# Second choices scattered during the expert stage, a fourth buffer for weight pieces, and counts made while PE sums

## The chip, the core and the metric

One core of a Trainium2 chip runs the whole program in one launch. The metric is the device time of an execution in microseconds; three runs of the kernel before took 1609.75, 1610.61 (the median) and 1611.9 us. One further execution was recorded by the hardware profiler; its rows are the ones shown here.

## The reference, cut to what matters

The input is x of shape (128, 256, 9, 9). A convolutional token mixer comes first and gives x again; it is not touched by the change. Then each of the 128*81 = 10368 tokens of 256 values goes through a mixture of experts with eight experts:

```python
t = _to_tokens(x)                                  # (128, 81, 256)
xf = _ln_t(t).reshape(n, 256)                      # n = 10368
probs = softmax(xf @ Wr.T + br)                    # 8 experts
top2_prob, top2_idx = top_k(probs, 2)
comb = zeros((n, 8)).at[arange(n)[:, None], top2_idx].add(top2_prob)
h = gelu(einsum('nd,edh->enh', xf, W1) + b1, approximate=False)   # hidden 512
o = einsum('enh,ehd->end', h, W2) + b2
t = t + einsum('ne,end->nd', comb, o)
```

Only the two chosen experts of a token count, so the kernel computes 20736 rows rather than 8*10368.

## The kernel before, in words

Each engine has its own program; they meet in semaphores. After the mixer (up to about 734 us) two stages follow that the change touches, and a last one that adds the two results of each token (from 1503 us).

**Routing stage.** A pixel q (0 to 80) is a block of 128 tokens, one for each image. The pixels go in batches of 6, six times 12, and 3 (`BATCHES`, `FIRST`), and every engine walks the batches j = 0 to 7. PE turns two pixels (a pair) at a time and multiplies them with the router (`turn_pair`); ACT writes the turned pair back (`turned`, L1385); DVE makes its statistics (`pixel_parts`, L1050), the variance (`pixel_variance`), the logits and the two choices (`choice_logits`, `choices`, which ends with L1112, the counts of the batch per expert). PE sums these counts over the 128 images (`places`), and DVE makes of them the position of each token in its expert's region (`positions`: L1120 adds the base, L1122 adds pixel after pixel, L1129 and L1130 write the integer indices). ACT then normalises the pixel's rows into one of 18 ring slots (`row`, L1414 and L1416), and POOL scatters that slot twice into `rows_d` in DRAM, once by the first choice and once by the second (L1549). A row has 256 values and a tag of four words (position, token, weights).

In the same stage the weights come in: 32 pieces of 128x512. SP loads a piece into one of three buffers (L381), ACT rounds it to a high half (`high_piece`, L1423), DVE makes the low half (`low_piece`, L1042), which frees the buffer. In batch j ACT rounds piece 4j after `deviations`, and pieces 4j+1 to 4j+3 at the batch's end; as there are three buffers, 4j+3 can only be loaded when low piece 4j, the last thing DVE does in the batch, is done.

At the end DVE makes a table with the row start and the expert of each of 88 tiles of 256 rows (L1156 to L1180), SP writes a tile of empty rows behind each region (L387, L389), and SP, DVE wait for all scatters (`scat0` to `scat17`) before a tile is read.

**Expert stage.** For each of the 88 tiles SP loads 256 rows (`load_rows`, L400) into one of two slots, as soon as PE has turned the tile two before (`tt_p`) and DVE has copied its tags (`tag_c`, L1196, after the result of two tiles before, L1231). PE turns the rows (L685), multiplies up (L701) and down (L716); it is one tile ahead with the up product. ACT makes high halves (L1458) and gelu (L1466), DVE low halves (L1190, L1223) and the result (L1231), ACT weights it (L1473), and POOL scatters it to its tokens with two indirect DMAs (`return_rows`, L1558). The result has two slots: DVE waits for the return of two tiles before (`yst`), ahead of L1204.

Of the kernel before, what the change touches and what calls it, by code (L numbers as in the profile page):

```python
# [55 lines left out]
def metaformer_kernel(nc, x, taps, tap_bn, tap_rows, toeplitz_mask, ident, band_masks, rot_masks, zstrings,  # L56
# [14 lines left out]
    with ctx:  # L71
# [14 lines left out]
        y_d = dram("y_d", [2 * TOKENS, C])  # L86
        u_d = dram("u_d", [HW, 128, 136])
# [48 lines left out]
        def take_aux(parts, *dims, dt=fp32):  # L136
# [9 lines left out]
            if len(dims) > 1:  # L146
# [61 lines left out]
        stage_s = pool_[:, stage_at:stage_at + 3 * PIECE].rearrange("p (a n) -> p a n", a=3)  # L208
# [3 lines left out]
        base_s = sb("base_s", [128, EXPERTS])  # L212
# [3 lines left out]
        til_s = sb("til_s", [128, 4, EXPERTS])  # L216
# [9 lines left out]
        hot_s = take_aux(128, 3, WIDEST, EXPERTS)  # L226
        top_s = take_aux(128, 5, WIDEST)
        tot_s = take_aux(128, EXPERTS)
        at_s = take_aux(128, WIDEST, EXPERTS)
        pick_s = take_aux(128, 2, WIDEST, EXPERTS)  # L230
        tab_s = take_aux(1, 4, TILES)
        tcmp_s = take_aux(1, 2, TILES, EXPERTS)
# [5 lines left out]
        hh_s = take_aux(128, 2, 2, KB, SLOTS, dt=fp16)  # L238

# [6 lines left out]
                   l2_p l2m_c e_c band_p x1_c phase_a wst_in0 wst_in1 wst_in2 whi_c wlo_c b2_in rm_p rw_c  # L246
                   blk_p part_c turned_c lgr_c var2_c ln_c rstd_c nmr_c probs_c ex2_c tot_c tri_p xft_c idx_c
                   """ + " ".join(f"scat{k}" for k in range(RING)) + """ yw_c ends_c base_c pad_out tab_r rin0 rin1 tt_p xhi_c xlo_c h_p
# [13 lines left out]
        def landed(q):  # L262
            return 32 * (q // RING + 1)
# [15 lines left out]
        def _(sp):  # L279
# [97 lines left out]

            for n in range(PIECES):
                if n >= 3:
                    sp.wait_ge(S["wlo_c"], n - 2)  # L380
                sp.dma_start(stage_s[:, n % 3], ffn_w[n]).then_inc(S[f"wst_in{n % 3}"], 16)  # L381
# [10 lines left out]
            for k in range(RING):  # L392
                sp.wait_ge(S[f"scat{k}"], landed(HW - RING + (k - HW) % RING))
            sp.wait_ge(S["base_c"], 1)
# [8 lines left out]

            load_rows(0, 0)
            load_rows(1, 1)
            for t in range(2):
                sp.wait_ge(S["tt_p"], t + 1)
                sp.wait_ge(S["tag_c"], t + 1 + CREDIT)
                load_rows(t + 2, t)
            with sp.Fori(1, TILES // 2 - 1) as i:  # L410
                for par in range(2):
                    t = i * 2 + par
                    sp.wait_ge(S["tt_p"], t + 1)
                    sp.sem_inc(S["settle_s"], 1)
                    sp.wait_ge(S["tag_c"], t + 1 + CREDIT)
                    load_rows(t + 2, par)
# [20 lines left out]
        def _(pe):  # L437
# [224 lines left out]
            def places(j):  # L662

                pe.wait_ge(S["tot_c"], j + 1)
                nc.tensor.matmul(ps[:, 7, 0:EXPERTS], before_s[:, :], tot_s[:, :], start=True, stop=True)  # L665
                nc.tensor.matmul(ps[:, 7, EXPERTS:2 * EXPERTS], ones_s[:, :], tot_s[:, :],
                                 start=True, stop=True).then_inc(S["tri_p"], 1)
# [85 lines left out]
        def _(dve):  # L753
# [280 lines left out]
            link(nc.vector.tensor_copy(base_s[:, :], region_s[:, :]))  # L1034

            def low_piece(n):

                if n < 0 or n >= PIECES:
                    return
                dve.wait_ge(S["whi_c"], n + 1)  # L1040
                cols = slice(n * PIECE, (n + 1) * PIECE)
                nc.vector.scalar_tensor_tensor(w_s[:, 1, cols], stage_s[:, n % 3], WSCALE, w_s[:, 0, cols],  # L1042
                                               ALU.mult, ALU.subtract).then_inc(S["wlo_c"], 1)
# [43 lines left out]
            def choices(j):  # L1087
# [23 lines left out]
                link(nc.vector.tensor_tensor(hot_s[:, 2, 0:n, :], hot_s[:, 0, 0:n, :], hot_s[:, 1, 0:n, :], ALU.add))  # L1111
                nc.vector.reduce_sum(tot_s[:, :], hot_s[:, 2, 0:n, :].rearrange("p s e -> p e s"),  # L1112
                                     axis=AX.X).then_inc(S["tot_c"], 1)

            def positions(j):

                lo, hi = FIRST[j], FIRST[j + 1]
                n = hi - lo
                dve.wait_ge(S["tri_p"], j + 1)
                link(nc.vector.tensor_tensor(at_s[:, 0, :], base_s[:, :], ps[:, 7, 0:EXPERTS], ALU.add))  # L1120
                for s in range(n - 1):
                    link(nc.vector.tensor_tensor(at_s[:, s + 1, :], at_s[:, s, :], hot_s[:, 2, s, :], ALU.add))  # L1122
                start(nc.vector.tensor_tensor(base_s[:, :], base_s[:, :], ps[:, 7, EXPERTS:2 * EXPERTS], ALU.add))
                for k in range(2):
                    ins = nc.vector.tensor_tensor(pick_s[:, k, 0:n, :], at_s[:, 0:n, :], hot_s[:, k, 0:n, :], ALU.mult)
                link(ins)
                nc.vector.reduce_sum(ptag_s[:, lo:hi, 0], pick_s[:, 0, 0:n, :], axis=AX.X)
                link(nc.vector.reduce_sum(top_s[:, 0, 0:n], pick_s[:, 1, 0:n, :], axis=AX.X))
                nc.vector.tensor_copy(idx_s[:, 0, lo:hi], ptag_s[:, lo:hi, 0])  # L1129
                nc.vector.tensor_copy(idx_s[:, 1, lo:hi], top_s[:, 0, 0:n]).then_inc(S["idx_c"], 1)  # L1130
# [6 lines left out]
            for j in range(len(BATCHES)):  # L1137
                pixel_parts(j + 1, 0)
# [13 lines left out]
            nc.vector.tensor_copy(tili_s[:, 1, :], base_s[:, :]).then_inc(S["ends_c"], 1)  # L1152
            for n in range(4 * len(BATCHES) - 3, PIECES):
                low_piece(n)
            cnt, tiles, ends = (til_s[:, k, :] for k in range(3))
            link(nc.vector.tensor_tensor(cnt, base_s[:, :], region_s[0:128, :], ALU.subtract))  # L1156
            link(nc.vector.tensor_scalar(cnt, cnt, float(SLOTS - 1), None, ALU.add))
            link(nc.vector.tensor_copy(tili_s[:, 0, :], cnt))
            link(nc.vector.tensor_scalar(tili_s[:, 0, :], tili_s[:, 0, :], SLOTS.bit_length() - 1, None,
                                         ALU.arith_shift_right))  # L1160
            link(nc.vector.tensor_copy(tiles, tili_s[:, 0, :]))
            link(nc.vector.tensor_copy(ends, tiles))
            for e in range(1, EXPERTS):
                link(nc.vector.tensor_tensor(ends[:, e:e + 1], ends[:, e:e + 1], ends[:, e - 1:e], ALU.add))


            full = [1, TILES, EXPERTS]
            link(nc.vector.tensor_tensor(tcmp_s[:, 0], ends[0:1, :].unsqueeze(1).to_broadcast(full),
                                         turn_s[:, :].unsqueeze(2).to_broadcast(full), ALU.is_le))
            link(nc.vector.tensor_tensor(tcmp_s[:, 1], tcmp_s[:, 0], tiles[0:1, :].unsqueeze(1).to_broadcast(full), ALU.mult))  # L1170
            nc.vector.reduce_sum(tab_s[:, 0, :], tcmp_s[:, 0], axis=AX.X)
            link(nc.vector.reduce_sum(tab_s[:, 1, :], tcmp_s[:, 1], axis=AX.X))
            nc.vector.tensor_scalar(tab_s[:, 2, :], tab_s[:, 0, :], float(EXPERTS), float(SLOTS), ALU.is_lt, ALU.mult)
            link(nc.vector.tensor_tensor(tab_s[:, 1, :], turn_s[:, :], tab_s[:, 1, :], ALU.subtract))
# [6 lines left out]

            for k in range(RING):
                dve.wait_ge(S[f"scat{k}"], landed(HW - RING + (k - HW) % RING))
            dve.wait_ge(S["pad_out"], 16 * (EXPERTS + 1))
# [87 lines left out]
        def _(act):  # L1272
# [134 lines left out]
            def row(j, q):  # L1407
# [4 lines left out]
                if q >= RING:  # L1412
                    act.wait_ge(S[f"scat{slot}"], landed(q - RING))
                nc.scalar.activation(xf_s[:, slot, 0:C], pixel_block(q), ACT.Identity,  # L1414
# [3 lines left out]
            def high_piece(n):  # L1418

                if n >= PIECES:  # L1420
                    return
                act.wait_ge(S[f"wst_in{n % 3}"], 16 * (n // 3 + 1))
                nc.scalar.activation(w_s[:, 0, n * PIECE:(n + 1) * PIECE], stage_s[:, n % 3], ACT.Copy,  # L1423
# [6 lines left out]
            for j in range(len(BATCHES)):  # L1430
                pairs = pairs_of(j + 1, 0) + pairs_of(j + 1, 1)
                left = list(range(FIRST[j], FIRST[j + 1]))
                for pair in pairs[:BANKS - 1]:
                    turned(pair)
                for pair in pairs[BANKS - 1:]:
# [11 lines left out]
                for n in range(4 * j + 1, 4 * j + 4):  # L1447
                    high_piece(n)
            for n in range(4 * len(BATCHES), PIECES):
# [48 lines left out]
        def _(pool):  # L1498
# [47 lines left out]
            for q in range(HW):  # L1546
                pool.wait_ge(S["xft_c"], q + 1)
                for k in range(2):
                    nc.gpsimd.indirect_dma_start(  # L1549
                        out=rows_d[:, :], out_offset=bass.IndirectOffsetOnAxis(ap=idx_s[:, k, q:q + 1], axis=0),  # L1550
                        in_=xf_s[:, q % RING, :], in_offset=None).then_inc(S[f"scat{q % RING}"], 16)
# [10 lines left out]
            with pool.Fori(0, TILES // 2) as i:  # L1562
# [99 lines left out]
```

## Time and profile before

| | us |
|---|---|
| median of three runs | 1610.61 |
| profiled execution, its time | 1601.33 |
| its span, first to last instruction | 1599.6 |
| routing stage in it | 734 to 985 |
| expert stage in it | 985 to 1503 |

In the span PE is busy 81%, DVE 68%, ACT 48%, POOL 36%. These are means over stages with different limits, so the rows that matter are those of one stage, one batch or one tile. A line of a timeline gives the start, the time from there to the end, engine, line, operation, destination and sources, the number of instructions merged, and in brackets the idle time of the engine before it with what ended it. Most timeline durations overlap the next instruction by some 0.1 us.

### The profile page before, as it was taken

What the parts mean: (1) busy time and instruction counts of PE and PEld (TensorE: products, weight loads), DVE (VectorE), ACT (ScalarE), POOL (GpSimd) and SP (SyncE); (2) the same over time, 40 slices, a digit from 0 to 9 for tenths busy, and PEclk for the clock granted to TensorE, in tenths of its full rate; (3) what the DMA queues carried; (4) which work ended last, traced back from release to release, by engine and by line L of the source; (5) the groups of instructions that cost most, each with busy time, mean ns of one, the idle gap of its engine ahead of it and who ended that gap; (6) DMA issues with size and microseconds to landing.
All of it is one profiled execution on the core that took longest, in us unless ns stands there. A gap on an engine that the chain in (4) does not pass through costs nothing.

```text
span 1599.6 us, 36879 instructions
## 1 busy us (share of the span) xinstructions
PE 1297.4 (81%) x9796; PEld 1072.9 (67%) x9797; DVE 1080.9 (68%) x2553; ACT 771.0 (48%) x1828; POOL 568.3 (36%) x561
## 2 busy tenths in 40 slices
PE   0197999999999999977656403999999999999592
PEld 0196999857676666657556302888888888888441
DVE  6797555378878788884656662777777777777462
ACT  0295666455444544442677761544555555555200
POOL 0163111333444334430577773333333333333200
PEclk9998999999999999985555555999999999999897
DMA  8635783858877978741243453222222222222297
GB/s 325 143 89 225 304 320 135 246 140 187 190 183 179 209 175 192 178 105 47 82 151 130 150 192 114 89 83 87 92 93 93 85 90 93 89 87 77 99 424 310
DMA packets 256214, 251.16 MB, mean 157 GB/s; under 512 B 149753, under 2 KB 234190, under 8 KB 251876
## 3 DMA queue, kind: packets, MB, share of 16 engines
q1 hardware_dynamic: 235789, 197.20, 41.1%
q0 software_dynamic: 20320, 53.45, 9.7%
q8 instruction: 18, 0.29, 0.1%
q14 instruction: 21, 0.17, 0.0%
q10 hardware_dynamic: 66, 0.05, 0.0%
HBM read 152.34 MB, written 105.75 MB: 161 GB/s over the span
## 4 chain that ended last, share of the span: by engine, by line
PE 56%; DVE 16%; DMA 10%; issue 6%; ACT 4%; SPq 3%; POOL 2%; DVEq 1%; ACTq 0%; POOLq 0%
PE ps L716 15%; PE ps L701 14%; PE ps L520 5%; PE ps L500 4%; PE ps L539 3%; DMA u_d<-in_zstrings 3%; PE ps L685 2%; DMA pool_<-k_d 2%; DMA pool_<-y_d 2%; POOL rows_d L1549 2%; PE ps L566 2%; SPq L291 2%; DMA pool_<-in_ffn_w 2%; PE ps L489 2%; ACT aux L1414 2%
## 5 line engine op out<-in xcount | busy, mean ns | idle before, releaser
L1558 POOL DMA_INDIRECT y_d<-pool_,to_s x176 | 173.5, 986 | 357.3 <-ACT pool_ L1473 328.0
L716 PE MATMUL ps<-pool_,aux 128*128 x2112 | 246.9, 273 | 4.9 <-DVE aux L1223 3.2
L701 PE MATMUL ps<-aux,pool_ 128*128 128x256 f16 x2112 | 247.1, 274 | 0.8 <-ACT aux L1466 0.6
L716 PEld LDWEIGHTS ps<-pool_,aux 128*128 128x128 f16 x2112 | 199.0, 98 | 47.4 <-issue 23.6
L701 PEld LDWEIGHTS ps<-aux,pool_ 128*128 x2112 | 207.2, 98 | 25.6 <-issue 1.4
L1549 POOL DMA_INDIRECT rows_d<-aux,idx_s x162 | 158.6, 979 | 105.7 <-ACT aux L1416 60.8
L1466 ACT ACTIVATE aux<-ps,b_s 128x256 f32<-128x256 f32 x352 | 138.1, 474 | 92.6 <-DVE aux L1223 92.5
L1458 ACT ACTIVATE aux<-ps 128x512 f16<-128x512 f32 x88 | 52.5, 597 | 187.0 <-PE ps L685 187.0
L1543 POOL DMA_DIRECT2D pool_<-v_d x64 | 50.0, 781 | 214.6 <-PE ps L599 213.2
L1231 DVE SCALAR_TENSOR_TENSOR pool_<-ps,pool_ 128x512 f32<-128x512 f32 x88 | 60.8, 691 | 92.4 <-PE ps L716 92.4
L539 PE MATMUL ps<-pool_,se_w_s 81*81 81x512 f32 x256 | 115.5, 593 | 3.6 <-DMA pool_<-k_d 3.6
L1223 DVE TENSOR_TENSOR aux<-aux 128x1024 f16<-128x1024 f32 x88 | 107.8, 1225 | 3.1
L1371 ACT ACTIVATE pool_<-ps,pool_ 128x81 f32<-128x81 f32 x256 | 79.5, 336 | 52.1 <-DVE pool_ L932 52.1
L883 DVE COPY aux<-ps 81x512 f32<-81x512 f32 x64 | 44.0, 687 | 71.5 <-PE ps L500 71.4
L685 PE MATMUL ps<-ident_s,pool_ 128*128 128x128 f32 x352 | 53.9, 276 | 44.1 <-DMA pool_<-rows_d 44.1
L520 PE MATMUL ps<-pool_,aux 82*128 82x162 f32 x512 | 85.6, 309 | 0.0
L1050 DVE BATCH_NORM_STATS2 aux<-big 128x6 f32<-128x256 f32 x81 | 45.0, 603 | 58.7 <-ACT big L1385 58.7
L665 PE MATMUL ps<-aux,before_s 128*128 128x8 f32 x16 | 4.8, 371 | 97.2 <-DVE aux L1112 97.2
L1473 ACT ACTIVATE pool_<-pool_,wrow_s 128x256 f32<-128x256 f32 x176 | 78.9, 498 | 9.1 <-DVE pool_ L1231 9.1
L1359 ACT ACTIVATE pool_<-ps,sa_ab 128x324 f32<-128x324 f32 x64 | 39.7, 620 | 86.6 <-PE ps L551 86.6
L1525 POOL COPY aux<-big 128x324 f32 x64 | 29.2, 457 | 138.6 <-PE ps L500 129.0
L1190 DVE TENSOR_TENSOR aux<-ps,aux 128x512 f16<-128x512 f32 x88 | 60.1, 683 | 24.8 <-ACT aux L1458 24.8
(204 smaller groups left out, 2974.4 us busy)
## 6 DMA issues: line engine op xcount, KB each, us to landing
pool_<-rows_d SPq DMA_DIRECT2D x88, 260.0 KB
pool_<-y_d SPq DMA_DIRECT2D x18, 1152.0 KB, 12.9
big<-in_x SPq DMA_DIRECT2D x2, 5184.0 KB, 21.2
xn_d<-big SPq DMA_DIRECT2D x8, 1296.0 KB, 4.8
v_d<-aux SPq DMA_DIRECT2D x64, 162.0 KB, 2.5
ks_d<-aux SPq DMA_DIRECT2D x64, 162.0 KB, 3.1
pool_<-xn_d SPq DMA_DIRECT2D x32, 324.0 KB
pool_<-k_d SPq DMA_DIRECT2D x32, 324.0 KB
```

What stands on the lines that cost most here:

```text
L500: last = nc.tensor.matmul(ps[0:HW, 4 + par, c * BS:(c + 1) * BS], xq_s[:, par, c, :], ident_s[:, :], start=True, stop=True)
L520: last = nc.tensor.matmul(o, pt_s[:, par, c, :], m_s[:, side, k * QUAD + c, :, :] .rearrange("p v n -> p (v n)"), start=True, stop=True)
L539: last = nc.tensor.matmul(ps[0:HW, n, :], se_w1_s[:, k, :], kq_s[:, par, k, 2 * n:2 * n + 2, :].rearrange("p b j -> p (b j)"), start=k == ...
L685: last = nc.tensor.transpose(ps[:, par, h * SLOTS + s * 128:h * SLOTS + (s + 1) * 128], rin_s[:, par, s, h * 128:(h + 1) * 128], ident_s[: ...
L701: last = nc.tensor.matmul(o, w_s[:, a, bass.ds(e * (4 * PIECE) + (k * HID + j * 128), 128)], xh_s[:, par, b, k * SLOTS:(k + 1) * SLOTS], s ...
L716: last = nc.tensor.matmul(ps[:, 6 + par, s * C:(s + 1) * C], hh_s[:, par, a, j, s * 128:(s + 1) * 128], w_s[:, b, bass.ds(e * (4 * PIECE) ...
L1223: nc.vector.tensor_tensor(lo, hf_s, hi, ALU.subtract).then_inc(S["hlo_c"], 1)
L1371: ins = nc.scalar.activation(e_s[:, par, h, b, :], ps[:, 2 + h, b * HW:(b + 1) * HW], ACT.Exp, bias=sm_s[:, par, 2, j:j + 1], accum_out=sm ...
L1466: nc.scalar.activation(hf_s[:, j * SLOTS:(j + 1) * SLOTS], ps[:, 2 + 2 * par + j // 2, (j % 2) * SLOTS:(j % 2 + 1) * SLOTS], ACT.Gelu, bia ...
L1473: ins = nc.scalar.activation(yo_s[:, par, s, :], yo_s[:, par, s, :], ACT.Copy, scale=wrow_s[:, par, s:s + 1])
L1549: nc.gpsimd.indirect_dma_start(out=rows_d[:, :], out_offset=bass.IndirectOffsetOnAxis(ap=idx_s[:, k, q:q + 1], axis=0), in_=xf_s[:, q % RI ...
L1558: nc.gpsimd.indirect_dma_start(out=y_d[:, :], out_offset=bass.IndirectOffsetOnAxis(ap=to_s[:, par, k:k + 1], axis=0), in_=yo_s[:, par, k, ...
```

## The change

Four things change. (1) In the routing stage POOL scatters each pixel by its first choice only, and SP also copies the rows, three pixels at a time, to a DRAM tensor `xrow_d` (`keep_rows`). The second choices get their places behind the first choices of their expert. In the expert stage the tiles are ordered so that tiles with first choices only come first; there are at least 33 of them (`SURE`). During these SP loads the kept rows back, three pixels at a time into two buffers (`load_late`), and POOL scatters them between its returns. (2) There are four buffers for weight pieces; ACT rounds pieces 4j-3 to 4j-1 after the third turned pair, and only 4j after `deviations`. (3) Positions are counted for first and second choices apart, 16 columns wide, and the sums within a batch are made before the wait for PE. (4) The table has 16 groups (full tiles of first choices, then the rest), and a pass over all pixels then adds to each second position the number of first choices of its expert (`idx2f_c`), before DVE lets PE start (`tab_r`).

```diff
+STAGED = 4
+THIRD = 3
+LATE = HW // THIRD
+SURE = -(-(BS * HW - EXPERTS * (SLOTS - 1)) // SLOTS)
+        def late_before(t):
+            return min(HW, 2 * THIRD + (HW - 2 * THIRD) * t // (SURE - 4))
+        def late_turn(b):
+            return 1 + min(t for t in range(SURE) if late_before(t) >= (b - 1) * THIRD)
...
@@ SP, routing stage @@
-            for n in range(PIECES):
-                if n >= 3:
-                    sp.wait_ge(S["wlo_c"], n - 2)
+            def load_piece(n):
+                if n >= STAGED:
+                    sp.wait_ge(S["wlo_c"], n - STAGED + 1)
...
+            def keep_rows(q):
+                sp.wait_ge(S["xft_c"], q + THIRD)
+                slot = q % RING
+                sp.dma_start(xrow_d[q:q + THIRD].rearrange("q b c -> b q c"),
+                             xf_s[:, slot:slot + THIRD, :]).then_inc(S[f"rst{slot // THIRD}"], 16)
+            for j in range(len(BATCHES)):
+                for n in range(4 * j, 4 * j + 4):
+                    load_piece(n)
+                for q in range(FIRST[j], FIRST[j + 1], THIRD):
+                    keep_rows(q)
@@ SP, expert stage @@
+            def load_late(b):
+                if b >= 2:
+                    sp.wait_ge(S[f"late_out{b % 2}"], b // 2 * (16 * THIRD))
+                sp.dma_start(late_s[:, b % 2], xrow_d[b * THIRD:(b + 1) * THIRD].rearrange("q b c -> b q c")
+                             ).then_inc(S[f"late_in{b % 2}"], 16)
+            def next_rows(t, par):
+                sp.wait_ge(S["tt_p"], t + 1)
+                sp.sem_inc(S["settle_s"], 1)
+                sp.wait_ge(S["tag_c"], t + 1 + CREDIT)
+                load_rows(t + 2, par)
             load_rows(0, 0)
             load_rows(1, 1)
+            sp.wait_ge(S["idx2f_c"], 1)
+            for b in range(2):
+                load_late(b)
+            for t in range(SURE - 2):
+                next_rows(t, t % 2)
+                for b in range(2, LATE):
+                    if late_turn(b) == t:
+                        load_late(b)
+            for k in range(2):
+                sp.wait_ge(S[f"late_out{k}"], 16 * THIRD * len(range(k, LATE, 2)))
...
@@ DVE, positions @@
+                start(nc.vector.memset(at_s[:, 0], 0.0))
+                link(nc.vector.tensor_copy(at_s[:, 1], hot_s[:, :, 0, :]))
+                for s in range(1, n - 1):
+                    link(nc.vector.tensor_tensor(at_s[:, s + 1], at_s[:, s], hot_s[:, :, s, :], ALU.add))
+                pixel_parts(j + 1, 0)
                 dve.wait_ge(S["tri_p"], j + 1)
...
@@ DVE, behind the table @@
+            wide = [128, HW, EXPERTS]
+            link(nc.vector.tensor_tensor(spread_s, pos2_s[:, :].unsqueeze(2).to_broadcast(wide),
+                                         region_s[:, :].unsqueeze(1).to_broadcast(wide), ALU.is_ge))
+            link(nc.vector.tensor_tensor(spread_s, spread_s, starts[:, full_ones].unsqueeze(1).to_broadcast(wide), ALU.mult))
+            link(nc.vector.reduce_sum(moved, spread_s, axis=AX.X))
+            link(nc.vector.tensor_tensor(moved, moved, pos2_s[:, :], ALU.add))
+            nc.vector.tensor_copy(idx_s[:, 1, :], moved).then_inc(S["idx2f_c"], 1)
...
@@ ACT @@
                 for pair in pairs[:BANKS - 1]:
                     turned(pair)
+                for n in range(4 * j - 3, 4 * j):
+                    high_piece(n)
                 for pair in pairs[BANKS - 1:]:
...
-                for n in range(4 * j + 1, 4 * j + 4):
-                    high_piece(n)
@@ POOL @@
             for q in range(HW):
                 pool.wait_ge(S["xft_c"], q + 1)
-                for k in range(2):
...
+            pool.wait_ge(S["idx2f_c"], 1)
+            sent = 0
+            for t in range(SURE - SURE % 2):
+                for q in range(sent, late_before(t)):
+                    b = q // THIRD
+                    pool.wait_ge(S[f"late_in{b % 2}"], 16 * (b // 2 + 1))
+                    nc.gpsimd.indirect_dma_start(
+                        out=rows_d[:, :], out_offset=bass.IndirectOffsetOnAxis(ap=idx_s[:, 1, q:q + 1], axis=0),
+                        in_=late_s[:, b % 2, q % THIRD, :], in_offset=None).then_inc(S[f"late_out{b % 2}"], 16)
+                sent = late_before(t)
+                return_rows(t, t % 2)
```

## Rows read from the trace of the kernel before

**Rows 1.** Busy time by stretches: us, engine busy (instructions), granted clock, DMA share, GB/s.

```profile
853.00:882.00 29.00, 16.22 (x76) 15.82 (x76) 18.33 (x70) 20.82 (x40) 22.17 (x23) 0.50 0.42 142
...
1100.00:1130.00 30.00, 29.96 (x271) 26.05 (x270) 22.19 (x54) 15.69 (x38) 9.84 (x10) 1.00 0.27 88
```

**Rows 2.** The chain of waits in order of time: start, us, what.

```profile
979.16 2.43 DMA rows_d<-aux,idx_s
...
982.88 0.42 SPq L400
```

**Rows 3.** Timeline of PE, its first expert tile.

```profile
985.55 1.08 PE L685 MATMUL ps<-ident_s,pool_ 128*128 128x128 f32 x4 [43.69 <-DMA pool_<-rows_d]
```

**Rows 4.** The scatters' source line: ns min/median/max, first and last start; their landing.

```profile
L1549 POOL DMA_INDIRECT rows_d<-aux,idx_s x162: 956/960/1365, 759.8 to 979.2; - x162
...
DMA to landing us min/median/max: 2.4/2.4/4.6
```

**Rows 5.** Timeline of DVE, the counts that end a batch's choices.

```profile
751.23 0.24 DVE L1112 TENSOR_REDUCE aux<-aux 128x8 f32<-128x48 f32 x1
...
776.50 0.32 DVE L1112 TENSOR_REDUCE aux<-aux 128x8 f32<-128x96 f32 x1
...
805.35 0.32 DVE L1112 TENSOR_REDUCE aux<-aux 128x8 f32<-128x96 f32 x1
...
922.11 0.32 DVE L1112 TENSOR_REDUCE aux<-aux 128x8 f32<-128x96 f32 x1
...
940.60 0.18 DVE L1112 TENSOR_REDUCE aux<-aux 128x8 f32<-128x24 f32 x1
```

**Rows 6.** Timeline of ACT: rows, turned pairs and roundings.

```profile
758.65 0.80 ACT L1414 ACTIVATE aux<-big,aux 128x256 f32<-128x256 f32 x1
...
761.15 0.80 ACT L1414 ACTIVATE aux<-big,aux 128x256 f32<-128x256 f32 x1
...
780.16 0.63 ACT L1423 ACTIVATE pool_<-pool_ 128x512 f16<-128x512 f32 x1 [7.12 <-DMA pool_<-in_ffn_w]
...
793.17 1.06 ACT L1385 ACTIVATE big<-ps 128x512 f32<-128x512 f32 x1
...
945.36 1.67 ACT L1423 ACTIVATE pool_<-pool_ 128x512 f16<-128x512 f32 x3
```

**Rows 7.** Timeline of DVE, the tile table.

```profile
955.51 0.16 DVE L1156 TENSOR_TENSOR til_s<-base_s,region_s 128x8 f32<-128x8 f32 x1
...
956.74 1.39 DVE L1164 TENSOR_TENSOR til_s<-til_s 128x1 f32<-128x1 f32 x7
...
958.16 0.88 DVE L1168 TENSOR_TENSOR aux<-til_s,turn_s 1x704 f32<-1x704 f32 x1
```

**Rows 8.** Source line L399, the read of a tile's row start.

```profile
L399 SPq TENSOR_LOAD <-tabi_s x88: 262/270/290, 982.1 to 1483.8; - x88
```

**Rows 9.** Timeline of SP, the empty rows behind the regions.

```profile
952.91 9.28 SPq L387 DMA_DIRECT2D rows_d<-aux  x8
```

**Rows 10.** Timeline, POOL's first return, and all engines in one later tile.

```profile
1003.13 1.00 POOL L1558 DMA_INDIRECT y_d<-pool_,to_s  x1 [23.02 <-ACT pool_ L1473]
...
1102.39 2.81 PE L716 MATMUL ps<-pool_,aux 128*128 x24
...
1106.25 0.90 ACT L1473 ACTIVATE pool_<-pool_,wrow_s 128x256 f32<-128x256 f32 x2
...
1106.77 1.22 DVE L1223 TENSOR_TENSOR aux<-aux 128x1024 f16<-128x1024 f32 x1
...
1107.00 0.40 SPq L400 DMA_DIRECT2D pool_<-rows_d  x1
...
1108.03 0.98 POOL L1558 DMA_INDIRECT y_d<-pool_,to_s  x1 [3.62 <-ACT pool_ L1473]
...
1108.15 2.81 PE L716 MATMUL ps<-pool_,aux 128*128 x24
```

**Rows 11.** Source line L1204: ns min/median/max, first and last start.

```profile
L1204 DVE TENSOR_SCALAR here_s<-tag_s,region_s x88: 217/492/506, 996.7 to 1503.0; 128x2 f32<-128x2 f32 x88
```

More of the change, by code:

```diff
@@ L393, in _ @@
                 sp.wait_ge(S[f"scat{k}"], landed(HW - RING + (k - HW) % RING))
+            for g in range(RING // THIRD):
+                sp.wait_ge(S[f"rst{g}"], kept(g))
             sp.wait_ge(S["base_c"], 1)
@@ L1151, in _ @@
             nc.vector.tensor_copy(zero_s[:, :, C + 1:C + 2], pad_s[:, :].unsqueeze(2))
-            nc.vector.tensor_copy(tili_s[:, 1, :], base_s[:, :]).then_inc(S["ends_c"], 1)
+            firsts, starts, ends, weighted = (til_s[:, k, :] for k in range(4))
+            full_ones, rest = slice(0, EXPERTS), slice(EXPERTS, 2 * EXPERTS)
+            last_row = ends[:, full_ones]
+            link(nc.vector.tensor_tensor(firsts[:, full_ones], base_s[:, 0], region_s[0:128, :], ALU.subtract))
+            link(nc.vector.tensor_tensor(last_row, base_s[:, 1], firsts[:, full_ones], ALU.add))
@@ L1153, in _ @@
+            nc.vector.tensor_copy(tili_s[:, 1, :], last_row).then_inc(S["ends_c"], 1)
             for n in range(4 * len(BATCHES) - 3, PIECES):
                 low_piece(n)
[L1155 to L1160, printed above, removed]
@@ L1170, in _ @@
[L1170 to L1174, printed above, removed]
+            counts = weighted[:, full_ones]
@@ new lines, in _ @@
+            link(nc.vector.tensor_tensor(counts, last_row, region_s[0:128, :], ALU.subtract))
+            link(nc.vector.tensor_scalar(counts, counts, float(SLOTS - 1), None, ALU.add))
+            for value, tiles in ((firsts[:, full_ones], starts[:, full_ones]), (counts, starts[:, rest])):
+                link(nc.vector.tensor_copy(tili_s[:, 0, :], value))
+                link(nc.vector.tensor_scalar(tili_s[:, 0, :], tili_s[:, 0, :], SLOTS.bit_length() - 1, None,
+                                             ALU.arith_shift_right))
+                link(nc.vector.tensor_copy(tiles, tili_s[:, 0, :]))
@@ new lines, in _ @@
+            link(nc.vector.tensor_tensor(starts[:, rest], starts[:, rest], starts[:, full_ones], ALU.subtract))
+            link(nc.vector.tensor_copy(ends, starts))
+            for e in range(1, 2 * EXPERTS):
+                link(nc.vector.tensor_tensor(ends[:, e:e + 1], ends[:, e:e + 1], ends[:, e - 1:e], ALU.add))
+            link(nc.vector.tensor_scalar(weighted, starts, -1.0, None, ALU.mult))
+            behind = slice(EXPERTS - 1, 2 * EXPERTS - 1)
+            link(nc.vector.tensor_tensor(weighted[:, behind], weighted[:, behind], starts[:, full_ones], ALU.add))
@@ new lines, in _ @@
+            behind, one_less = slice(EXPERTS, 2 * EXPERTS - 1), slice(0, EXPERTS - 1)
+            link(nc.vector.tensor_tensor(weighted[:, behind], weighted[:, behind], starts[:, one_less], ALU.subtract))
+            full = [1, TILES, 2 * EXPERTS]
+            link(nc.vector.tensor_tensor(tcmp_s, ends[0:1, :].unsqueeze(1).to_broadcast(full),
+                                         turn_s[:, :].unsqueeze(2).to_broadcast(full), ALU.is_le))
+            link(nc.vector.reduce_sum(tab_s[:, 0, :], tcmp_s, axis=AX.X))
@@ L1446, in _ @@
                     row(j, q)
[L1447 to L1449 removed]
+            for n in range(4 * len(BATCHES) - 3, PIECES):
                 high_piece(n)
```

105 lines of the change are left out of this document (56 added, 49 removed).

## Prediction, made before the changed kernel ran

> **What bounds the kernel now.** I read the busy time by stretches first, then the chain of waits, then single batches and tiles. Two stages concern the change. In the routing stage (about 733 to 985 us) POOL is the full engine: in 29 us it runs 23 scatters, one per 1.26 us, which is one of 0.96 us and a gap of 0.3, while PE, at granted clock 0.50, ACT and DVE have idle time [rows 1]. It has 162 to run, the last begins at 979.16, lands 2.43 later, and the first expert tile is on PE at 985.55 [rows 2 to 4]. The rows themselves are made faster: choices end (the end of L1112, called T below) at 751.47, 776.82, 805.67, ..., 922.43 and 940.78, so 145.6 us for five batches of twelve [rows 5]. The expert stage is PE's: 271 matmuls in 30 us, 52 a tile, is 5.76 us a tile with PE busy throughout [rows 1]. The profiled execution took 1601.33 us, its span of 1599.6 and 1.7 around it that the change does not touch; the median of the runs is 1610.61, 9.3 above; I sum differences in the profiled one and take them off the median.
>
> **Routing, the loop.** Before, after T a batch goes: a low piece that frees a buffer, the load of the next weight piece, and ACT, idle for it, rounds it from 780.16 to 780.79, T+3.97; only then pairs are turned, places counted, rows made. The last pair is turned at 794.23, T+17.4, and from there to the next T it is 11.44 [rows 5, 6]. After, a fourth buffer means pieces 4j-3 to 4j were loaded in the batch before, so ACT does not wait. It turns pair one before T, and pairs two and three as PE delivers them; the batch that has no such wait shows the third done at T+7.18 (758.65 less 751.47) [rows 5, 6]. Then come the three roundings, 1.67, then three times two rows and a pair, 2.50 each (758.65 to 761.15) [rows 6]. 7.18+1.67+7.50 = 16.35, so 1.1 earlier. The counts now run while PE sums, but that is off the path: a low piece, the sums of one batch, the statistics of a pair, offsets and picks, by the small operations' 0.2 each and some 1.1 for the statistics an estimated 5.9, put the indices at T+5.9, and ACT asks for them at T+8.9. One add of 0.29 less and a reduce twice as wide (estimated +0.16) give -0.13. Five batches: 16.35+11.44-0.13 = 27.66 each, 138.3, against 145.6: **-7.3**. Bounds: 0 if the roundings cost all that the wait did; -15 if they fall into ACT's gaps and PE's delivery sets the pace. The value lies between because they sit behind the third pair, where ACT has no gap left. To the last batch (922.43 to 940.78) nothing is rounded ahead of the first pair any more, and few rows follow: the T+3.97 counts nearly whole, **-3.9**.
>
> **Routing, the end.** Before, from 940.78 to 985.55 it is 44.8 us, and POOL's remaining scatters set it. After, POOL's 81 scatters need 102 us (81 times 1.26) in a stage of over 200, and its last follows the last row by a few us. What is late next is ACT, then DVE. From T of the last batch: ACT still has ten rows of the batch before (0.80 each [rows 6], done at T+4.7), three roundings, two rows, a rounding, a row, three roundings: T+11.1. DVE fills its zeros and makes the last low pieces until T+12.6. Then the tile table: six small operations took 1.23 (955.51 to 956.74), seven chained sums 1.39, and passes over 1x704 0.88 each [rows 7]. After, 13 small ones make 2.6, 15 sums 3.1, four passes over 1x1408, about 1.72 each, 6.9, and ten small ones behind them 2.0: 14.6. So the table is ready at T+27.2. The new places of the second choices (three passes over 648, estimated 0.8 each from the 704 ones, and four small operations: 3.4) and some 26 passed waits (about 1) come before DVE releases PE: T+31.6. SP's path is shorter: the load takes 0.8 to issue (982.1 to 982.88) and 2.67 to reach PE [rows 2, 3, 8], T+30.7. The pads also move out of POOL's cover: nine issues, eight of them 9.28 us [rows 9], from T+10.8 and a landing near 2.9 end at T+24.5, 2.7 before they would count. 44.8-31.6 = **-13.2**. Bounds -9 (pads and rows slower) to -17. Routing in all -7.3-3.9-13.2 = **-24.4**.
>
> **Expert stage.** The 81 second scatters come back here: six before the first tile, 75 over the next 29, 2.6 a tile, and SP issues 27 loads of three rows between its own. The six hide before the first results: POOL's first return came 17.6 us after PE's first tile (1003.13) [rows 10]. Per tile POOL then has two returns and 2.6 scatters, 4.6 times 1.27 = 5.84, against PE's 5.76: just full, with a lag of a few us that the two-tile slot of the results can absorb. The price is in SP's queue. A late load waits until the three scatters that read its buffer have landed, and the next tile's rows stand behind it on SP. Take 0 at the end of PE's second product of a tile, 1105.20 [rows 10]. ACT weights until 1107.15, +1.95; POOL wakes 0.28 later (written out, with constant waits; in the loop it is 0.88, 1107.15 to 1108.03), and two returns take 2.55: the first late scatter starts at +4.8. Landing 2.4 [rows 4]: the first, second or third scatter of the tile has landed at +7.2, +8.5 or +9.7. SP then issues the late load (0.4), the next tile's load (0.8), and PE has the rows 2.67 later: +11.1, +12.4, +13.6, and some 0.2 more as 390 KB go ahead of it. Before, this load was issued at 1.80 (1107.00) of its own tile, +7.6. PE needs the rows at two tiles, +11.5. So PE is late by 0, 1.1 or 2.3, where the first, second or third scatter completes a buffer; by the diff's late_before and late_turn that is 9, 10 and 4 times among 23 loads, and once (+2) at the end, where SP waits for all. If each counts whole: 11+9+2 = 22. If the lateness is shared by the three tiles that the loop spans: 7+2 = 9. Runs of two or three such loads follow each other, so most is shared: I take **+14**. The operation is not in the trace, so the ends are wider: 0 if landing and issue overlap better than the rows say, 32 if a scatter lands in 4.6, the longest of the 162 [rows 4].
>
> A port cost is possible too. DVE's L1204 takes 492 ns in most tiles and 217 at best [rows 11], and POOL's return begins just before it (1108.03) in each tile. On DVE's way from one product to the next lies the cast L1221 before L1223, which ends at 1107.99, 0.16 before PE's next product at 1108.15 [rows 10]. Up to two operations there, delayed 0.275 each, less 0.16, over 29 tiles, would be 11 us; 0 if it falls into PE's stalls, which give DVE room. I take 0. The Trainium skill, "SBUF — State Buffer", section "Who interferes with whom", says that DVE's casts and copies in their two-port mode and GpSimd hold the shared port exclusively, one fully blocking the other. The step of L1204 agrees with a wait of that sort; by the page the cast would meet POOL in most tiles, since POOL is busy nearly all the time, and the sum would be nearer the 11 than the 0. It is a rival below.
>
> **Sum.** -24.4+14 = -10.4; 1610.6-10.4 = **1600** us.
>
> **Rivals.** (A) SP's waits cost nearly nothing: PE finds its rows, the expert stage is as before, up to 2 us: 1588. For it: nine of the loads need only the first scatter; against it: the sum of +12.4 against 11.5 has no spare. (B) Slower: the scatters land later. Place: SP's wait ahead of each late load. Each 0.1 of landing adds about 0.8 us to the stage (29 tiles, shared by three), so at 3.8 instead of 2.4 it has eaten the routing gain; at 4.6 the stage costs 32, and the time is 1618. For it: rows, late rows, scatters and returns then share the DMA engines, and one scatter did take 4.6; against it: the median was 2.4 with the engines over 0.4 busy. (C) The port: DVE's cast waits for POOL in most tiles, +11 on top: 1611. For it L1204's step; against it: DVE gains room wherever PE waits for rows. (D) The routing loop gains nothing since ACT, not POOL, was its bound, and only the end shortens: -17+14, 1608.
>
> **How the numbers follow.** Forecast 0.52, its own range 1594 to 1606; A 0.20; B 0.12; C 0.08; D 0.08. This kernel's runs differ by 2 us, so 0.2% (3.2 us) is about what can be told from no change. Faster (below 1607.4): the forecast, A, and a part of D, 0.76. Same: the rest of D, C and an edge of B, 0.12. Slower: B and some of C, 0.12. The range of 8 in 10 leaves out the better half of A and the worse half of B: 1587 to 1612.
>
> **What would show it.** Right: POOL no longer full in the routing stage, five batches in about 138 us, ACT without waits on weight loads, PE's first tile near 961; in the first 33 tiles SP waiting on the late scatters, PE's transposes waiting on DMA for some 14 us in all, and none after. Wrong: a first tile after 970 (the end is bound elsewhere); no PE waits in the expert stage (A); waits of PE on L1223's successor instead of on rows (C); scatters landing in 3.5 or more (B).

## The result and the profile after

The changed kernel took 1630.05 us (median of four runs, 1628.05 to 1630.29), the kernel before 1611.26 beside it (median of four): ratio 1.0111, interval 1.0093 to 1.0129. It is slower by 1.1%; the prediction was 1600 and "faster".

The profiled span of the changed kernel is 1628.4 us. The change does not touch the mixer, yet the first batch's counts behind it come up to 11 us earlier or later from one profiled run to the next. So stages are compared here, not totals, and a second profile of the kernel before (span 1607.8) stands beside the first. All times in this table are differences of row starts, in us: from the first batch's counts to PE's first expert tile, then from the first transpose of one tile to that of another, and at last from tile 87 to the end of the span.

| | routing | tiles 0 to 4 | 4 to 30 | 30 to 34 | 34 to 87 | behind | span |
|---|---|---|---|---|---|---|---|
| before | 234.3 | 20.3 | 151.4 | 23.4 | 308.0 | 110.9 | 1599.6 |
| before, second profile | 234.8 | 20.2 | 152.2 | 23.2 | 309.6 | 112.4 | 1607.8 |
| after | 209.9 | 20.5 | 189.8 | 29.8 | 310.8 | 112.8 | 1628.4 |

The routing stage gives 24.9 against the second profile, where 24.4 was forecast. The expert stage up to tile 34 takes 44.5 more, where 14 was forecast; all else is 1.1. That sums to the 20.6 between the two spans. Most of it lies in tiles 4 to 30 and 30 to 34, which are bounded by these transposes on PE's timeline, first in the second profile of before, then after:

```profile
1010.35 0.60 PE L685 MATMUL ps<-ident_s,pool_ 128*128 128x128 f32 x4
...
1162.60 0.60 PE L685 MATMUL ps<-ident_s,pool_ 128*128 128x128 f32 x4
...
1185.83 0.60 PE L685 MATMUL ps<-ident_s,pool_ 128*128 128x128 f32 x4
```

```profile
985.22 0.60 PE L734 MATMUL ps<-ident_s,pool_ 128*128 128x128 f32 x4
...
1175.02 0.65 PE L734 MATMUL ps<-ident_s,pool_ 128*128 128x128 f32 x4 [1.31 <-DMA pool_<-rows_d]
...
1204.83 0.60 PE L734 MATMUL ps<-ident_s,pool_ 128*128 128x128 f32 x4
```

Routing first. By stretches (us, engine busy (instructions), granted clock, DMA share, GB/s), POOL has 11.62 instead of 22.17 in the same 29 us, and it is the expert stage where it is now loaded, at 19.94 instead of 9.84 in 30 us [rows 1]:

```profile
853.00:882.00 29.00, 16.22 (x76) 15.82 (x76) 20.29 (x84) 21.34 (x41) 11.62 (x12) 0.50 0.47 151
1100.00:1130.00 30.00, 25.55 (x215) 20.17 (x212) 16.29 (x41) 12.27 (x28) 19.94 (x20) 1.00 0.57 178
```

PE got through 215 matmuls there, not 271. The counts on DVE's timeline (start, us, line) come every 27.46, with 14.37 to the last batch [rows 5]:

```profile
754.75 0.32 DVE L1160 TENSOR_REDUCE aux<-aux 128x16 f32<-128x96 f32 x1
...
862.16 0.48 DVE L1160 TENSOR_REDUCE aux<-aux 128x16 f32<-128x192 f32 x1
...
917.10 0.49 DVE L1160 TENSOR_REDUCE aux<-aux 128x16 f32<-128x192 f32 x1
...
931.47 0.21 DVE L1160 TENSOR_REDUCE aux<-aux 128x16 f32<-128x48 f32 x1
```

PE's first tile follows 33.2 behind, and what releases it is DVE, no longer a load of rows that waits on POOL's scatters [rows 3]:

```profile
964.68 1.12 PE L734 MATMUL ps<-ident_s,pool_ 128*128 128x128 f32 x4 [31.91 <-DVEq L1264]
```

Then the waits from 965 to 1210 (engine and line, what it waited for: us in total, times, longest):

```profile
SPq L439 <- DMA rows_d<-aux,idx_s: 144.0, 25, 7.7
SPq L431 <- DVE tag_s L1274: 33.9, 9, 7.0
SPq L444 <- DMA rows_d<-aux,idx_s: 8.4, 1, 8.4
...
PE ps L734 <- DMA pool_<-rows_d: 17.8, 17, 3.2
PE ps L750 <- issue: 14.0, 23, 0.9
```

L439 is the late load: SP stands ahead of it for scatters in all of its 25 waits. PE then waits 17.8 for rows, and 14.0 more in 23 pieces of up to 0.9 ahead of the up product. The up product uses the tile turned one turn before, so it does not wait for these transposes. What comes late with them is PE's own reading of the tile's expert number (L740, `value_load`): on time it starts 0.9 ahead of the transposes (984.3, transposes at 985.22), and in a late tile behind their start (998.5, transposes at 998.38), so that its 0.3 us and the steps behind it stand in the open:

```profile
L740 PEldq TENSOR_LOAD <-tabi_s x1: 303/303/303, 984.3 to 984.3; - x1
...
L740 PEldq TENSOR_LOAD <-tabi_s x1: 303/303/303, 998.5 to 998.5; - x1
```

Twice PE's granted clock also fell here for some 3 us from 1.00, which is 2.4 GHz, to the lower level, 1.2 GHz (0.50 in 1030 to 1032, 0.53 in 1178 to 1180). Ahead of the first fall PE had waited 3.21 us for rows, ahead of the second 1.31 and 0.79; behind a wait of 2.92 that ended at 1198.16 the clock stayed at 1.00. The two up products took 3.87 and 4.45 us instead of 2.79, so some 2.7 of the 44.5:

```profile
1030.87 3.87 PE L750 MATMUL ps<-aux,pool_ 128*128 128x256 f16 x24 [0.20 <-issue]
...
1176.46 4.45 PE L750 MATMUL ps<-aux,pool_ 128*128 128x256 f16 x24 [0.79 <-issue]
```

One turn of the loop, from the timelines of PE, ACT, POOL and SP:

```profile
998.38 0.65 PE L734 MATMUL ps<-ident_s,pool_ 128*128 128x128 f32 x4 [1.43 <-DMA pool_<-rows_d]
999.65 2.79 PE L750 MATMUL ps<-aux,pool_ 128*128 128x256 f16 x24 [0.61 <-issue]
...
1013.18 0.65 PE L734 MATMUL ps<-ident_s,pool_ 128*128 128x128 f32 x4 [0.77 <-DMA pool_<-rows_d]
...
999.16 0.60 ACT L1537 ACTIVATE aux<-ps 128x512 f16<-128x512 f32 x1 [3.43 <-PE ps L734]
999.65 0.90 ACT L1552 ACTIVATE pool_<-pool_,wrow_s 128x256 f32<-128x256 f32 x2
...
1001.45 1.00 POOL L1636 DMA_INDIRECT y_d<-pool_,to_s  x1 [0.86 <-issue]
1002.75 1.00 POOL L1636 DMA_INDIRECT y_d<-pool_,to_s  x1 [0.30 <-issue]
1004.05 0.97 POOL L1646 DMA_INDIRECT rows_d<-aux,idx_s  x1 [0.30 <-issue]
1005.33 0.96 POOL L1646 DMA_INDIRECT rows_d<-aux,idx_s  x1 [0.31 <-issue]
...
1007.77 0.38 SPq L439 DMA_DIRECT2D aux<-xrow_d  x1
1009.19 0.39 SPq L432 DMA_DIRECT2D pool_<-rows_d  x1
```

The transposes at 998.38 are late; two returns and two late scatters follow on POOL, the second starts at 1005.33 and has landed when SP goes on at 1007.77; the tile's rows are issued only at 1009.19 and used at 1013.18. That is 14.8 us for two tiles, 7.4 each instead of 5.8. The chain of waits (start, us, what) runs through the same pieces:

```profile
1005.33 2.42 DMA rows_d<-aux,idx_s
1007.77 0.38 SPq L439
...
1009.19 3.87 DMA pool_<-rows_d
1013.05 0.13 issue
1013.18 0.65 PE ps L734 x4
```

So the scatters land as fast as was assumed (2.41 to 2.65 in this chain, up to 1210), but the rows take 3.87 from issue behind the late load, not 2.67. From 985 to 1200 such a load lands in 3.7 (median), and in 2.8 behind tile 34. Whether the late load ahead of it or the scatters beside it cost this was not taken apart.

### The profile page after: what moved, and what is told of

Same layout as the page of the kernel before. It is cut to its first block, busy times and chain, and to the rows that moved or that the text cites. A ratio compares the mean times of both kernels' runs of the same rounds, so it can differ in the third digit from the quotient of the medians.

```text
span 1628.4 us, 36837 instructions
## 1 busy us (share of the span) xinstructions
PE 1312.9 (81%) x9796; PEld 1075.0 (66%) x9797; DVE 1088.2 (67%) x2579; ACT 772.9 (47%) x1828; POOL 575.3 (35%) x561
## 4 chain that ended last, share of the span: by engine, by line
PE 53%; DMA 15%; DVE 14%; issue 6%; ACT 5%; SPq 4%; POOL 0%; DVEq 0%; ACTq 0%; POOLq 0%
PE ps L765 12%; PE ps L750 12%; PE ps L568 5%; PE ps L548 4%; DMA pool_<-rows_d 3%; DMA u_d<-in_zstrings 3%; PE ps L587 2%; DMA rows_d<-aux,idx_s 2%; DMA pool_<-y_d 2%; PE ps L734 2%; DMA aux<-u_d 2%; PE ps L614 2%; DMA pool_<-k_d 2%; SPq L309 2%; ACT aux L1493 2%
## 5 line engine op out<-in xcount | busy, mean ns | idle before, releaser
L1537 ACT ACTIVATE aux<-ps 128x512 f16<-128x512 f32 x88 | 52.6, 597 | 214.4 <-PE ps L734 214.4
L1627 POOL DMA_INDIRECT rows_d<-aux,idx_s x81 | 79.5, 981 | 147.4 <-ACT aux L1495 130.9
L1646 POOL DMA_INDIRECT rows_d<-aux,idx_s x81 | 85.4, 1054 | 46.6 <-issue 25.6
L1552 ACT ACTIVATE pool_<-pool_,wrow_s 128x256 f32<-128x256 f32 x176 | 78.8, 498 | 10.8 <-DVE pool_ L1309 10.8
L734 PEld LDWEIGHTS ps<-ident_s,pool_ 128*128 128x128 f32 x352 | 41.0, 143 | 56.4 <-DVEq L1264 32.0
L694 PEld LDWEIGHTS ps<-router_s,big 128*128 128x128 f32 x324 | 75.9, 318 | 1.2 <-DVE big L1015 1.2
```

The lines of the kernel that those rows point to most:

```text
L734: last = nc.tensor.transpose(ps[:, par, h * SLOTS + s * 128:h * SLOTS + (s + 1) * 128], rin_s[:, par, s, h * 128:(h + 1) * 128], ident_s[: ...
L1552: ins = nc.scalar.activation(yo_s[:, par, s, :], yo_s[:, par, s, :], ACT.Copy, scale=wrow_s[:, par, s:s + 1])
L1627: nc.gpsimd.indirect_dma_start(out=rows_d[:, :], out_offset=bass.IndirectOffsetOnAxis(ap=idx_s[:, 0, q:q + 1], axis=0), in_=xf_s[:, q % RI ...
L1646: nc.gpsimd.indirect_dma_start(out=rows_d[:, :], out_offset=bass.IndirectOffsetOnAxis(ap=idx_s[:, 1, q:q + 1], axis=0), in_=late_s[:, b % ...
```

## Experiments

The theories in the quoted expectations: S, SP's wait for late scatters ahead of a tile's rows; P, POOL cannot fit two returns and 2.6 scatters into a tile; D, the extra transfers slow the others down.

**The kernel before, once more.** Unchanged, for a second profile.

> The kernel before once more, for a second profile: its first profiled execution took 1601.33 us where its other runs took 1609.8 to 1614.5. Expected: routing from the first counts to the first expert tile again 234 us, PE's 88 tiles again 503 us; a span nearer 1609 would then have its surplus in the mixer or the last stage, which the change does not touch.

1609.48 us; its stages are the second row of the table above. They agree with the first profile within 1.6 us each. Its span is 8.2 us longer: 4.1 of it lie ahead of the first counts and 3.1 behind tile 34, so nearly all outside the stages compared here.

**Six late buffers.** Does SP's wait cost it?

```diff
-        late_s = take_aux(128, 2, THIRD, WIDE)
+        late_s = take_aux(128, LATE_SLOTS, THIRD, WIDE)      # LATE_SLOTS = 6
-            return 1 + min(t for t in range(SURE) if late_before(t) >= (b - 1) * THIRD)
+            return 1 + min(t for t in range(SURE) if late_before(t) >= (b - LATE_SLOTS + 2) * THIRD)
...
-            for b in range(2):
+            for b in range(LATE_SLOTS):
                 load_late(b)
```

> Six buffers for the late rows instead of two, so that a late load waits for scatters of tiles long past; same loads, same scatters. Theory S (SP's wait ahead of the late load holds back the next tile's rows): tiles 2 to 34, 232 us in the changed kernel and 188 before, fall to some 190 to 195, total about 1590. Rival P (POOL cannot do two returns and 2.6 scatters in a tile of 5.8, at 1.3 to 1.35 each and 0.5 to 0.9 to wake it needs 6.6): they fall to about 211 only, total about 1609. Rival D (the 390 KB loads and the scatters slow the rows' own loads on the DMA engines): no change, 225 to 232, total about 1628.

1612.25 us (median of ten, spread from 1601.55 to 1625.21; the profiled one took 1606.77), ratio to the kernel before 1.0032 (0.9995 to 1.0068): not to be told from no change. Tiles 4 to 30 take 162.1 (986.54 to 1148.64), down from 189.8, against 152.2 before: SP's wait was worth 27.7 of the 37.6. Tiles 2 to 34 take 209.9, which is the number of P (about 211) and not that of S (190 to 195): the wait was the first bound, and behind it stands POOL. Routing is 209.7; tiles 0 to 4 take 25.2 since six loads now go ahead of tile 2's rows, and tiles 30 to 34 take 33.5. Busy time by stretches, and the waits from 965 to 1200:

```profile
1030.00:1060.00 30.00, 28.91 (x256) 24.56 (x256) 19.01 (x46) 14.64 (x35) 23.32 (x22) 1.00 0.63 192
1060.00:1090.00 30.00, 27.97 (x243) 23.14 (x242) 19.88 (x50) 14.38 (x34) 23.32 (x22) 1.00 0.64 191
```

```profile
SPq L453 <- DMA rows_d<-aux,idx_s: 61.7, 16, 5.5
SPq L457 <- DMA rows_d<-aux,idx_s: 11.0, 1, 11.0
...
DVE here_s L1296 <- DMA y_d<-pool_,to_s: 27.6, 19, 3.0
```

POOL runs 22 indirect DMAs in 30 us, one per 1.36 us, and DVE now waits for POOL's returns, which it did not in the kernel before. SP still waits 61.7 us for scatters, but nearly always with time to spare: between tiles 4 and 30 PE waits 0.5 us for rows. What is left is POOL's: 162.1/26 = 6.23 us a tile, for 4.6 indirect DMAs of 1.36. The one wait of 11.0 at L457 is the end, where SP waits for all late scatters.

**No late loads.** Do the 390 KB transfers slow anything (D), or is it POOL (P)? This kernel leaves out the second choices' rows, so only its stages are read, not its total.

```diff
-            for b in range(2):
-                load_late(b)
...
-                for b in range(2, LATE):
-                    if late_turn(b) == t:
-                        load_late(b)
```

> The late loads and SP's waits for them are gone; POOL makes all 81 late scatters, from two buffers of empty rows that DVE fills once. Left out: second choices get empty rows, and the last stage adds the first result twice. S and D: tiles 2 to 34 in 188 to 192 us. P: about 211, since POOL's work is the same. DVE's fill puts the first tile some 2 us later.

1609.93 us. Tiles 4 to 30 take 162.2, as with six buffers, and tiles 30 to 34 take 33.7. With POOL's work kept and the loads and SP's waits for them gone, the same 10 us stay, so the late loads' part in D is worth nothing and P holds: tiles 2 to 34 take 207.8, where P had about 211. What the scatters themselves cost the rows' loads was not taken out here. The waits from 965 to 1210:

```profile
SPq L444 <- DMA rows_d<-aux,idx_s: 12.5, 1, 12.5
...
DVE here_s L1282 <- DMA y_d<-pool_,to_s: 26.6, 13, 2.4
```

**Weighting ahead of the high halves.** In the loop above ACT weights a result only behind the high halves of a late tile (L1537, then L1552). Does that feed the lateness back?

```diff
-                    high_rows(t + 1, 1 - k)
                     weighed(t - 2, k)
+                    high_rows(t + 1, 1 - k)
```

> As the changed kernel, but ACT weights the result of two tiles before ahead of the high half of the newly turned rows, not behind it. If a late tile also delays its own remedy (turned rows late, so weighting late, so return late, so late scatters late, so SP's next wait longer), tiles 2 to 34 fall from 232 us to 205 to 220. If SP's wait stands alone, or the bound is P or D, they stay within 4 us of 232.

1634.25 us; tiles 4 to 30 take 187.3, tiles 2 to 34 231.2 against 232.4. The run with three buffers below has the expert stage of the changed kernel word for word and takes 192.4 and 234.6, so this difference is within what the stage varies. ACT's order is not part of the cause. POOL's idle time ahead of its returns falls from 61.0 to 48.7 us (965 to 1210) and the tiles come no faster; why was not followed further.

**Half of the second choices at once.** If S, P and the drain at the end are the whole of it, fewer late scatters over more tiles cure it. Of every six pixels the last three are again scattered by both choices in the routing stage, and counted in the first group; only the other three are kept.

```diff
-LATE = HW // THIRD
+LATE = (HW // THIRD + 1) // 2                                # 14
+KEPT = LATE * THIRD                                          # 42
...
-SURE = -(-(BS * HW - EXPERTS * (SLOTS - 1)) // SLOTS)
+SURE = -(-(BS * (2 * HW - KEPT) - EXPERTS * (SLOTS - 1)) // SLOTS)      # 53
...
+        def at_once(q):
+            return q // THIRD % 2 == 1
...
         def late_before(t):
-            return min(HW, 2 * THIRD + (HW - 2 * THIRD) * t // (SURE - 4))
+            return min(KEPT, 2 * THIRD + (KEPT - 2 * THIRD) * t // (SURE - 8))
         def late_turn(b):
-            return 1 + min(t for t in range(SURE) if late_before(t) >= (b - 1) * THIRD)
+            return 3 + min(t for t in range(SURE) if late_before(t) >= (b - 1) * THIRD)
...
+                link(nc.vector.tensor_copy(pick_s[:, :, 0:n, :], hot_s[:, :, 0:n, :]))
+                if n > THIRD:
+                    nc.vector.memset(once_of(pick_s[:, 1, 0:n, :], n), 0.0)
+                    link(nc.vector.tensor_tensor(once_of(pick_s[:, 0, 0:n, :], n), once_of(hot_s[:, 0, 0:n, :], n),
+                                                 once_of(hot_s[:, 1, 0:n, :], n), ALU.add))
...
+                for k in range(1 + at_once(q)):
```

> The change, but of every six pixels three are scattered by both choices in the routing stage and only the other three are kept for later: 42 late scatters instead of 81, and 53 tiles instead of 33 can go before the first tile with late rows, so 0.8 late scatters a tile (2.6 before). A late load is issued three turns behind the scatters that free its buffer, and the last late scatter is eight tiles ahead of the rows that wait for it. Theory S+P (the loss in the expert stage is SP's wait for late scatters, POOL being full, and the drain at the end): POOL has 2.8 times 1.27 = 3.6 us of work in a tile of 5.76, SP waits for nothing; tiles 4 to 30 take 152 (190 in the changed kernel), tiles 30 to 34 23.5 (29.8). In the routing stage POOL has 18 scatters in a batch, 22.7 us of a step of 27.5, and DVE three small operations more ahead of the counts (about 0.5 a batch): a gain of 20 to 24 stays. The whole: 1588 to 1594. Rival T (rows that come and go during the expert stage slow it whatever the order of waits): 0.4 us or more for each tile with late work, 17 to 20 in 45 tiles: 1605 to 1612. Rival Q (18 scatters with ACT's longer wait for ring slots make POOL the bound of the routing stage again): steps of the counts 29 as before, 1597 to 1600.

1586.54 us, ratio to the kernel before 0.9869 (0.9836 to 0.9902): it beats both kernels. Tiles 4 to 30 take 152.3, tiles 30 to 34 take 23.2, tiles 34 to 87 take 311.3: the expert stage is that of the kernel before. Routing is 211.7, a gain of 23.1 against the second profile; the counts come every 28.0 (805.89 to 917.90 for four), 0.5 later than in the changed kernel, as forecast for DVE's three more operations. Tiles 4 to 30 run from 984.27 to 1136.56. By stretches and waits (965 to 1300):

```profile
853.00:882.00 29.00, 16.22 (x76) 15.82 (x76) 20.41 (x78) 21.60 (x41) 18.96 (x19) 0.50 0.47 151
...
1100.00:1130.00 30.00, 29.71 (x267) 25.52 (x265) 21.71 (x54) 15.07 (x36) 14.51 (x15) 1.00 0.42 135
```

```profile
SPq L438 <- DVE tag_s L1292: 248.7, 56, 7.4
...
PE ps L757 <- DVE aux L1286: 0.8, 1, 0.8
```

In this stage SP waits for no scatter any more, but for the tile's tags, as in the kernel before, and PE's waits for rows are next to nothing (0.2 us in all). Both T and Q are out: T wanted 17 to 20 us more in the expert stage, Q counts every 29. Which of its three edits does most (fewer late scatters, the load three turns later, the earlier end) was not taken apart.

**The fourth buffer alone**, on the kernel before (part 2, both scatters in the routing stage), and **three buffers** in the changed kernel (all parts but 2, which is this edit taken back):

```diff
-                if n >= 3:
-                    sp.wait_ge(S["wlo_c"], n - 2)
+                if n >= STAGED:                                              # STAGED = 4
+                    sp.wait_ge(S["wlo_c"], n - STAGED + 1)
...
+                for n in range(4 * j - 3, 4 * j):
+                    high_piece(n)
                 for pair in pairs[BANKS - 1:]:
```

> The kernel before with part (2) alone: four weight buffers, three pieces rounded behind the third turned pair; both scatters stay in the routing stage. Theory R (POOL is the bound of the routing stage, ACT's wait for a weight piece lies in its shadow): counts end every 29 us as before, PE's first expert tile 234 us (within 2) after the first counts. Rival V (ACT's wait sets the step, POOL is full only because it is fed so): steps of 27.7 to 28, first tile 225 to 229 after the first counts.

> The changed kernel without part (2): three weight buffers, and the roundings in their old places. The prediction's sum (the wait for the first piece, 3.97 behind the counts, costs 1.1 a batch net of the three roundings): steps of 28.6 instead of 27.46, the last batch 18.3 instead of 14.4, first expert tile 219 to 221 after the first counts instead of 210. Rival R (POOL alone was the bound, part (2) adds nothing): steps of 27.5, 210. The expert stage as in the changed kernel, 232 for tiles 2 to 34.

The fourth buffer alone: 1615.34 us; counts every 27.6 as V said, yet the first tile 233.9 behind the first counts, as R said. Three buffers: 1634.94 us; counts every 27.0 and not 28.6, 16.7 to the last batch, and the first tile after 213.2. The waits in four batches of the fourth buffer alone (815 to 925), its first expert tile on PE's timeline, and the waits with three buffers (806 to 914):

```profile
ACT big L1386 <- PE ps L652: 23.1, 8, 4.4
...
POOL rows_d L1550 <- issue: 23.8, 78, 0.3
POOL rows_d L1550 <- ACT aux L1417: 2.7, 9, 0.3
```

```profile
996.10 1.08 PE L686 MATMUL ps<-ident_s,pool_ 128*128 128x128 f32 x4 [55.22 <-DMA pool_<-rows_d]
```

```profile
ACT pool_ L1502 <- DMA pool_<-in_ffn_w: 16.4, 4, 4.4
...
ACT aux L1493 <- DVE idx_s L1182: 3.6, 4, 1.2
...
POOL rows_d L1627 <- ACT aux L1495: 52.0, 16, 8.3
```

With four buffers and all scatters POOL is fed sooner and has no idle time but its gaps of 0.3. The last row is made 12.7 us earlier than in the second profile of before (185.9 instead of 198.6 behind the first counts), but the last scatter starts only 1.0 earlier (227.3 instead of 228.3): the rest goes into POOL's backlog, and PE's first tile again waits for rows behind POOL. With three buffers and half the scatters POOL waits for rows, ACT still waits 4.1 a batch for the weight piece, and the batch is no longer than 27.0 all the same; neither the prediction's 28.6 nor R's 27.5. So the split of the scatters, with the counts that come with it, is worth 21.6 of the 24.9 of routing, and the fourth buffer 3.3: 5.4 behind the seventh batch's counts (47.6 instead of 53.0 to the first tile), less 2.2 that it loses up to there.

## Why the prediction was wrong

- **What bounds the routing stage: right.** POOL was the full engine. The whole change shortens the stage by 24.9 (24.4 forecast), 21.6 of it without the fourth buffer; the fourth buffer alone shortens the batches and moves the end by 0.9. That the sum comes out so near is partly luck: the loop gives 1.0 more than forecast and the end 1.4 less.
- **The loop, -7.3: right in size, half right in cause.** Batches of 27.46 were forecast at 27.66. The fourth buffer alone does bring 27.6, as the sum has it, but here it was not needed: without it, with all other parts, batches take 27.0. I held the counts made while PE sums to be off the path. In the second profile of before, ACT waits up to 2.4 us for the indices in a batch; with three buffers in the changed kernel the longest such wait is 1.2 and the batches are 1.8 shorter than before. That points to the counts, though they were not tried by themselves. It is not POOL's backlog: with the fourth buffer alone POOL is full and the batches still take 27.6.
- **The last batch and the end, -3.9 and -13.2: right.** 14.37 (14.45 forecast by the same sum), and from the end of these counts 33.0, 1.4 more than forecast.
- **SP's queue, +14: the step that failed.** The stage up to tile 34 cost 44.5. "Runs of two or three such loads follow each other, so most is shared" took the lateness as spread over three tiles. The loop closes over two: transposes, the return of the last result, the scatters, the late load, and the rows of the tile after next. From the end of the product at 996.96 the second scatter had landed at +10.8 (+8.5 forecast) and the rows were used at +16.2 (+12.4), because in that turn ACT has weighted at +3.6 (+1.95; its order alone costs nothing, as the run with the other order shows), POOL comes to the return 0.9 behind (0.28), SP takes 1.42 from one load to the next (1.2), and the rows take 4.0 to PE (2.87). Six buffers take 27.7 us away.
- **POOL "just full, with a lag that the two-tile slot can absorb", 0: wrong.** 4.6 indirect DMAs were forecast at 5.84 us a tile, which is already 0.08 over PE's 5.76; with SP's wait gone POOL sets 6.2. This bound stands behind SP's wait: in the changed kernel POOL ran 20 in 30 us, in a full POOL it is 22. A slot absorbs a lag that comes and goes; an engine over its rate by 0.4 falls behind by that much in every tile, and 26 tiles make the 10 us that two experiments show.
- **The end, where SP waits for all late scatters, 2: too small.** The first tiles with late rows stand behind POOL's whole backlog: 6.6 us in tiles 30 to 34, and 10 in the two experiments where POOL was the bound.
- **Rival B** had the side and the place, SP's wait, but not the price: it wanted scatters that land in 3.8 or more, and those in the chain landed in 2.4 to 2.7. Even the upper bound of 32 fell short of 44.5: in the turn shown the rows come 3.8 later than was summed, though the landing is as assumed, and the end took 6.6 instead of 2.
- **Rivals A and D: out.** A wanted PE to find its rows; it waited 17.8 us for them. D wanted the batches to gain nothing; five of them took 137.3 instead of 145.6.
- **Rival C: no sign of it.** The cast takes 679/685/906 ns (least, median, most) over all tiles, 682/685/693 before; from 1000 to 1180, with POOL twice as busy, its mean is 688 and its longest 725. The step of 492 ns [rows 11] speaks even the other way, on average 234 there:

```profile
L1282 DVE TENSOR_SCALAR here_s<-tag_s,region_s 128x2 f32<-128x2 f32 x25 | 5.9, 234 | 2.2 <-issue 2.2
```

(In this view: busy us, mean ns, idle before.) In the kernel before, too, the step does not go with POOL's return: L1204 began 0.48 behind the start of one at 1096.87 and took 0.22 us, and 0.49 behind another at 1102.62 and took 0.49. The rule of the Trainium skill, "SBUF — State Buffer", section "Who interferes with whom", that casts in a two-port mode and GpSimd block each other, shows in no row here: the cast's median did not move, and in the expert stage up to 1210 PE waited for a DVE result once, for 0.4 us.

## What to carry to other kernels

Work moved off a full engine is only worth what the place it goes to can take: compare rates per tile, with each instruction's gap, and count an engine that comes out at its limit as over it. Here 5.84 against 5.76 became 6.23. A wait placed in the issuing engine's program ahead of loads that the bound engine needs should be met a whole loop ahead; here its latency was paid turn after turn. Where both sides are near full, split the work between them: half in each place, with the late loads issued later, made this kernel 1.3% faster, all of it in the second place 1.1% slower.

## What the runs showed of the hardware

- Two loads of 260 KB, issued by SP 1.2 and 1.4 us behind one of 390 KB, landed in 3.77 and 3.87 us; in the kernel before PE had such a load 2.67 us behind its issue.
- The first scatters, which share the routing stage with SP's copies of the rows, landed in 2.4/3.4/6.4 us (least, median, most), against 2.4/2.4/4.6 [rows 4]; PE's first tile waited for DVE and not for them.
- One late scatter held POOL for up to 1672 ns (median 965). In a full POOL one indirect DMA, return or scatter, took 1.36 us with its gap (22 in 30 us with six buffers; without the late loads 68 in 90 us, so 1.32), not the 1.26 of the routing stage.
